# Decoder layer on one core: early attention tiles kept at 32 keys through the value product, and the first cross-attention group prepared inside the feed-forward

## What is computed

```
x  = x + linear_attention(layernorm(x)) @ wo          # 16 heads of 8 features, elu+1 feature map
x  = layernorm(x + gelu_table(layernorm(x) @ w1) @ w2) # feed-forward 128-512-128
s  = where(query_masked or key > query, -1e9, q k^T / sqrt(8))   # q from x, k and v from the context
y  = layernorm(x + softmax(s) v @ WO)
out = layernorm(y + y Wshared + sum(top-2 gates) * (y Wexpert) + bias)
```

## Time and profile before

| | us |
|---|---|
| median of 3 runs | 604.05 (602.84 to 606.14) |
| the profiled execution | 608.8 |
| its span, first to last instruction | 607.1 |
| PE busy | 533.2 (88%) |
| DVE busy | 417.6 (69%) |
| ACT busy | 371.0 (61%) |
| POOL busy | 340.5 (56%) |
| TensorE's mean granted clock | 0.969 |

### The profile page before, as it was taken

One profiled execution on the slowest core, in us unless ns is written; L12 is line 12 of the kernel. 1 busy time (PEld: TensorE's weight loads), 2 busy tenths in 40 slices (PEclk: granted clock), 3 DMA queues, 4 the chain that ended last, 5 costly groups with the idle time before them and its releaser, 6 DMA issues.

```text
span 607.1 us, 23038 instructions
## 1 busy us (share of the span) xinstructions
PE 533.2 (88%) x9312; PEld 371.9 (61%) x9312; DVE 417.6 (69%) x1453; ACT 371.0 (61%) x643; POOL 340.5 (56%) x619
## 2 busy tenths in 40 slices
PE   2799999989999999888999999998989989999741
PEld 1477676756777777635666666666656656666530
DVE  2577777756677766345677797777876887779743
ACT  2365665647777777646666666676666756766521
POOL 6766666656755554531345546754575457544564
PEclk9899999999999999969999999999999999999876
DMA  6600000000000000011111111111111111101001
GB/s 170 181 32 2 3 1 3 3 2 1 1 2 1 2 1 2 9 25 29 32 31 29 42 30 49 39 35 28 49 49 25 27 49 48 28 25 32 20 19 35
DMA packets 24987, 17.97 MB, mean 30 GB/s; under 512 B 3121, under 2 KB 21425, under 8 KB 24881
## 3 DMA queue, kind: packets, MB, share of 16 engines
q1 hardware_dynamic: 24448, 16.43, 10.3%
q10 hardware_dynamic: 432, 0.07, 0.1%
HBM read 9.67 MB, written 4.19 MB: 23 GB/s over the span
## 4 chain that ended last, share of the span: by engine, by line
PE 61%; SPq 11%; issue 7%; POOL 6%; ACT 5%; DMA 5%; DVE 4%; POOLq 0%; DVEq 0%; ACTq 0%
SPq L391 11%; PE pair L1143 7%; PE pair L1127 7%; PE pair L1158 6%; PE pair L1177 6%; PE pair L1210 6%; PE pair L1018 5%; DMA k_exp<-k_sb 4%; PE pair L1096 4%; PE pair L1187 4%; PE pair L1109 3%; PE pair L1196 3%; PE pair L1089 3%; ACT gel L684 3%; PE pair L1165 2%
## 5 line engine op out<-in xcount | busy, mean ns | idle before, releaser
L684 ACT ACTIVATE gel<-pair 128x1024 f32<-128x1024 f32 x64 | 65.6, 1025 | 76.8 <-PE pair L1177 76.8
L908 DVE TENSOR_REDUCE neg_max<-pair 128x16 f32<-128x1024 f32 x64 | 60.9, 952 | 24.5 <-PE pair L1165 24.4
L1158 PE MATMUL pair<-k_exp,qT 64*32 64x256 f32 (+1 forms) x1024 | 58.1, 505 | 13.1 <-DMA k_exp<-k_sb 10.0
L1143 PEld LDWEIGHTS pair<-w,gel 128*128 128x128 f32 x512 | 60.7, 192 | 9.0 <-issue 7.2
L1187 PEld LDWEIGHTS pair<-v,gel 128*32 128x32 f32 x4096 | 41.5, 110 | 36.2 <-ACT gel L684 31.2
L1143 PE MATMUL pair<-w,gel 128*128 128x128 f32 x512 | 62.1, 275 | 1.0 <-ACT gel L650 1.0
L1187 PE MATMUL pair<-v,gel 128*32 128x18 f32 x4096 | 48.0, 187 | 14.1 <-ACT gel L684 11.3
L1127 PE MATMUL pair<-hT,w 128*128 128x512 f32 x128 | 58.5, 597 | 2.0 <-ACT lev L645 1.3
L678 ACT ACTIVATE gel<-gel,row_scale 128x512 f32<-128x512 f32 x80 | 54.4, 720 | 6.3 <-DVE gel L921 6.2
L300 POOL TENSOR_SCALAR veps_c<-mv_c 128x4 f32<-128x4 f32 x16 | 3.7, 230 | 95.4 <-issue 89.0
L1177 PE MATMUL pair<-ident,gel 128*128 128x128 f32 x384 | 52.5, 280 | 0.4 <-ACT gel L678 0.4
(11 more groups left out here) (126 smaller groups left out, 1236.7 us busy)
## 6 DMA issues: line engine op xcount, KB each, us to landing
X<-in_x SPq DMA_DIRECT2D x16, 256.0 KB, 3.0
cT<-in_ctx SPq DMA_DIRECT2D x16, 256.0 KB, 2.9
out_rows<-X SPq DMA_DIRECT2D x16, 256.0 KB, 2.6
k_exp<-k_sb SPq DMA_DIRECT2D x160, 16.0 KB
w<-in_L_attn_w SPq DMA_DIRECT2D x2, 256.0 KB, 3.5
w_kv<-in_L_attn_wk SPq DMA_DIRECT2D x1, 64.0 KB, 3.2
w_q<-in_L_attn_wq ACTq DMA_DIRECT2D x1, 64.0 KB, 3.0
w_kv<-in_L_attn_wv SPq DMA_DIRECT2D x1, 64.0 KB, 3.1
```

What stands on the lines that cost most here:

```text
L684: nc.scalar.activation(pT[par], pair[par][:, :, :].rearrange("p a c -> p (a c)"), ACT.Copy).then_inc(pT_ready, 1)
L908: nc.vector.tensor_reduce(neg_max[par][:, :].rearrange("p (a h) -> p a h", a=2), scores, AX.X, ALU.max, negate=True).then_inc(max_ready, 1)
L1143: last = nc.tensor.matmul(bank(6 + q)[:, P * t:P * (t + 1)], gel[:, q, f, P * t:P * (t + 1)], w_2[:, f, :], start=(f == 0), stop=(f == NF ...
L1158: nc.tensor.matmul(pair[t % 2][b * QW:(b + 1) * QW, half, 0:HH * width], qT[p][rows, batch + first:batch + first + QW], keys, start=True, ...
```

## The change

1. Odd tiles keep 32 keys for each head to the end. The turned probabilities are then 512 columns wide: four transposes and a 128x512 copy in place of eight and 128x1024. The value product takes four heads at a time (`v4`, 36 columns, 16 products). What masked queries owe to the later keys is one product over all heads (144 columns, four products) with a matrix `future`, which DVE makes from a mask row (`mask_rows`) that SP loads for each group. POOL no longer writes future keys; it copies the values of the first 32 keys into `v4` (`spread_v`, four copies a group).
2. The causal term of even tiles is added only to their last 32 keys.
3. PE transposes the rows of the feed-forward's result straight from `X`; POOL's copy of them (`copy_y`, L503) is gone. `yT` and `y2` get other memory.
4. The preparation of group 0 (keys, values, turned rows, queries, first scores) goes into the steps 11 to 15 of `phase2`, on bank 1. ACT's rows_a for the last groups move into the start of `phase3`.
5. In `phase1` DVE makes `phi_q` before `attend`.

```diff
+        v4 = [sb(f"v4{i}", [P, 2 * TG, QB, QB, HV]) for i in range(2)]
-        y2 = sb("y2", [P, TG, D])
+        y2 = xn[0]
...
+            def load_mask(g, p):
+                src = mask_early[2 * g:2 * g + 2, :].rearrange("n p -> (n p)")
+                sp.dma_start(mask_rows[p][:, :, :].rearrange("p n q -> p (n q)"),
+                             src.partition_broadcast(P)).then_inc(mask_loaded[p], 16)
...
                     load_ctx(s + 2, p)
+                if exists(s + 1) and s >= 0:
+                    after(sp, future_ready, s)
+                    load_mask(s + 1, 1 - p)
                 if exists(s - 2):
                     store(s - 2)
...
+            const(nc.gpsimd.memset(late_key[:, :], 0.0))
...
+                const(nc.gpsimd.memset(v4[i][:, :, :, :, :], 0.0))
+                for j in range(QB):
+                    const(nc.gpsimd.memset(v4[i][j * QW:(j + 1) * QW, :, :, j, DH:HV], 1.0))
...
             def phase3(s, p):
-                if exists(s):
-                    future_keys(2 * s + 1)
-                if exists(s + 2) and not early(s):
-                    copy_y(s + 2, p)
                 g, q = s + 1, 1 - p
                 if exists(g):
...
+                if exists(g):
+                    spread_v(g, q)
                 if exists(s - 2):
                     o = s - 2
                     ln_deviation(pool, ln_c, o, mv_c, veps_c, rstd_c)
...
-                nc.scalar.activation(pT[par], pair[par][:, :, :].rearrange("p a c -> p (a c)"),
-                                     ACT.Copy).then_inc(pT_ready, 1)
+                flat = pair[par][:, :, :].rearrange("p a c -> p (a c)")
+                nc.scalar.activation(pT[par], flat[:, 0:GW] if n % 2 else flat, ACT.Copy)\
+                    .then_inc(pT_ready, 1)
...
-            phase3(-1, 1, slots=(0, 1))
-            phase2(NG, 0)
-            phase3(-1, 1, slots=range(2, TG))
-            phase2(NG + 1, 1)
+            rows_a(NG - 3, 1)
+            probabilities(0)
+            rows_a(NG - 2, 0)
             act.wait_ge(down_done, NG)
-            pipeline(act, phase3, first=0, last=NG + 1)
+            phase3(0, 0, slots=(0,))
+            rows_a(NG - 1, 1)
+            phase3(0, 0, slots=range(1, TG))
+            pipeline(act, phase3, first=1, last=NG + 1)
...
-                if exists(s):
-                    attend(s, p)
                 if exists(g):
                     dve.wait_ge(expq_ready, g + 1)
                     after(dve, num_done, g - 1)
                     nc.vector.scalar_tensor_tensor(phi_q[q][:, :], bank(1), 1.0, expqk[q][:, 0, :],
                                                    ALU.add, ALU.max).then_inc(phiq_ready, 1)
+                if exists(s):
+                    attend(s, p)
...
+            def future_keys(g, q):
+
+                dve.wait_ge(mask_loaded[q], g // 2 * 16 + 16)
+                after(dve, pv_done, g * TG - TG)
+                nc.vector.tensor_scalar(future[q][:, :, :], mask_rows[q][:, :, :], 0.0,
+                                        late_key[:, 0:1], ALU.not_equal, ALU.mult)\
+                    .then_inc(future_ready, 1)
+
             def phase3(s, p, slots=range(TG)):
                 prev, old, q = s - 1, s - 2, 1 - p
                 for t in slots:
+                    if t == 2 and exists(s + 1):
+                        future_keys(s + 1, q)
...
+                if s == NG - 5:
+                    pe.wait_ge(projsb_ready, NG)
+                    pe.wait_ge(ctx_loaded[0], 16)
+                    project_qk(cT[0], w_xk, bank(1), xk_done)
+                if s == NG - 4:
+                    pe.wait_ge(k_ready, 1)
+                    project_v(0, 0)
+                if s == NG - 3:
+                    pe.wait_ge(v2_ready, 1)
+                    turn_y(0)
+                if s == NG - 2:
+                    pe.wait_ge(yT_ready, 1)
+                    project_qk(yT, w_xq, bank(1), xq_done)
+                if s == NG - 1:
+                    pe.wait_ge(const_ready, 3)
+                    pe.wait_ge(const_dve, 4)
+                    pe.wait_ge(h2T_ready, NG)
+                    first_scores(0, 0)
...
-                for i in range(HH):
+                for i in range(HH // 2 if n % 2 else HH):
                     if i % (HH // 2) == 0:
                         pe.wait_ge(exp_ready, shifted(n, 2 * i // HH))
...
+                if n % 2:
+                    pe.wait_ge(v4_ready, (n // TG + 1) * QB)
+                    pe.wait_ge(future_ready, n // TG + 1)
+                    for b in range(QB):
+                        nc.tensor.matmul(
+                            bank(7)[b * QW:(b + 1) * QW, 0:H * HV],
+                            future[p][:, t // 2, b * QW:(b + 1) * QW],
+                            v2[p][:, t // 2 * QB + b, :, :, :].rearrange("p i h e -> p (i h e)"),
+                            start=True, stop=False)
+                    for i in range(QB):
+                        for b in range(QB):
+                            last = nc.tensor.matmul(
+                                bank(7)[b * QW:(b + 1) * QW, QB * HV * i:QB * HV * (i + 1)],
+                                pT[1][:, P * i + b * QW:P * i + (b + 1) * QW],
+                                v4[p][:, t // 2 * QB + b, i, :, :].rearrange("p h e -> p (h e)"),
+                                start=False, stop=i == QB - 1)
```

More of the change, by code:

```diff
@@ L266, in up_bank, with first_bank @@
             return (6, 7, 2, 3)[f] if s == 0 else 2 + f
+        def first_bank(g, usual):
+            return 1 if g == 0 else usual
         def shifted(n, half):
@@ L378, in _ @@
             load_ctx(0, 0)
+            load_mask(0, 0)
             def spread_k(g, q):
@@ L494, in phase2, with spread_k @@
                     ln_offset(pool, ln_a, s - 1, mv_b, negm_b, rstd_b[1 - p], offs_b[1 - p])
-            def copy_y(g, p):
-                pool.wait_ge(ln_a.done, g + 1)
-                pool.wait_ge(h2_xposed, NG - 1 if isinstance(g, int) and g == 0 else NG)
-                after(pool, y_xposed, g - 1)
-                apart(pool)
-                nc.gpsimd.tensor_copy(y_in[p][:, :, :], X[:, tiles(g), :]).then_inc(y_copied, 1)
-            def spread_k(g, q, heads):
-                for h in heads:
+            def spread_k(g, q):
+                pool.wait_ge(k_ready, g + 1)
+                after(pool, s_done, g * TG - TG)
+                for h in range(HDMA, HH):
@@ L675, in probabilities @@
                     act.wait_ge(sub_ready, shifted(n, half))
[L676 to L677 removed]
+                    rows = probability_rows(n)
+                    part = rows if n % 2 else rows[:, GW * half:GW * (half + 1)]
                     nc.scalar.activation(part, part, ACT.Exp, scale=row_scale[:, n:n + 1])\
```

207 lines of the change are left out of this document (115 added, 92 removed).

## The result

The changed kernel takes 668.24 us (median of 4 runs, 665.32 to 670.66), the kernel before 605.1 us (median of 4, 602.84 to 610.29): a ratio of 1.1028, 95% interval 1.0943 to 1.1114. It is slower by 10%, where 2% faster (591.3 us) was forecast and 600 us was the upper end of the range. The profiled execution took 667.96 us and has a span of 666.2 us, against 608.8 and 607.1.

A forecast was written before the change was run, and what follows sets the result against it. Each stage had its own limit, cross-attention a closed loop of scores, DVE, POOL, store and ten DMAs. The terms 5.5 − 1.3 − 8.0 − 8.5 − 2.5 + 2 = −12.8 us against the 604.05 us median gave 591.3 us, range 582 to 600.

The forecast's parts named there:

- 0.3 us of mask row: Cross-attention step: DVE's added work for the mask row, priced at 0.3 us, with DVE still free before the scores are done.
- Fills, +5.5: Start: POOL's constant fills delay the first normalisation by 4.7 us, and PE's restart at the lower clock adds 0.8 us.
- `phi_q`, −1.3: Linear attention: making `phi_q` first saves at most 0.1 us in each of 13 steps, 1.3 us in all.
- Seam, −8.0: Feed-forward to cross-attention: 3.3 us of inserted PE work, then 26.4 us to group 1's first scores instead of 37.7.
- Cross-attention, −8.5: First scores of group 1 to those of group 15: 266.4 us where 274.96 us passed before.
- +2 for the clock: Cross-attention: two or three steps with a late DMA run PE at the lower clock, costing 2 us in all.
- PE's work, 17.0 to 17.1: Cross-attention step: PE needs 17.0 to 17.1 us, 2.0 us saved by cheaper odd and even tiles and a shorter wait.
- Tail, −2.5: After group 15's first scores: cheaper odd tiles, a smaller causal term and earlier expert products save 2.5 us.
- The loop is not closed: Rival, cross-attention: the store doesn't hold the DMAs back, steps follow PE at 17.1 us, 567 us in all; chance 0.07.
- The fills are hidden: Rival, start: something else holds the start, so 4.7 us less and no cold restart, 586 us; chance 0.13.
- The first group is not hidden: Rival, seam: late ACT or DVE, low clock or slower `weigh_values` loses 5 to 9 us, 596 to 600 us; chance 0.15.
- The lower clock in every step: Rival, cross-attention: PE restarts at 1.2 GHz after each key wait, steps take 21.0 us, 611 us in all; chance 0.10.

The follow-up runs named there:

- e1: Changed kernel with each group's mask rows loaded one step earlier; 598.71 us, ratio 0.9877 to the kernel before.
- e7: Kernel before with only `phi_q` put ahead of `attend` on DVE; 607.78 us, ratio 1.0018 to the kernel before.
- e3: e1 with the store of a group's result moved behind the ten key DMAs of the following step; 588.13 us, ratio 0.9701 to the kernel before.
- e5: e3 with POOL's fills of the value buffers spread over four steps of linear attention; 582.06 us, ratio 0.9620 to the kernel before.
- e8: e1 with eight key DMAs a step in place of ten; 584.94 us, ratio 0.9662 to the kernel before.
- e9: e5 with eight key DMAs a step in place of ten; 578.58 us, ratio 0.9541 to the kernel before.
- e12: Changed kernel, mask load left late, with DVE's `future_keys` moved from slot 2 to slot 3 behind the shift; 601.62 us, ratio 0.9929 to the kernel before.

## Why the prediction was wrong

The step that failed is one sentence: "SP's mask load stands behind the DMAs and ahead of a store that comes 12 us later". It asks who stands behind the load in SP's list, and prices it at nothing. It does not ask who waits for the load and what is queued behind that wait. The first time was to be had from rows of before: the list begins at the store and the ten DMAs take 6.8 us to issue, so a load behind them lands some 10 us after the store, an estimate (11.2 us in the change, 384.50 to 395.73). In e1, where it waits for nothing, DVE comes to `future_keys` 6.0 us after the store (399.12 to 405.11) or 7.6 (378.95 to 386.59), and the code had it at the head of slot 2, with the shifts behind it. I gave DVE "0.3 us of mask row" and looked at its duration alone. So the wait for the mask rows was put at nothing, and it measured 59.2 us in 15 waits; without it the same kernel is 69.5 us faster (e1). No rival had this case, and the chance of 0.09 for slower had other reasons.

Point by point, with the profiled executions (before to change; e1 where the late load hides a term):

- *Fills, +5.5, and `phi_q`, −1.3.* The last step of linear attention, PE's products with a wait of 1.26 us for ACT, starts at 133.28 in before, at 138.16 in the change: +4.9 (forecast +4.2). The normalisation of group 2 was where forecast, PE's transposes at 28.95 after 6.20 us. `phi_q` gave 0, since ACT's chain to `hT`, and 0.15 us from there to PE, had been the bound all along (e7).
- *Seam, −8.0.* From last `up` products to first scores of group 1: 26.9 us (forecast 26.4). Together with 3.15 us of inserted work (forecast 3.3): −7.6. Right.
- *Cross-attention, −8.5 and +2 for the clock.* First scores of group 1 to those of group 15: 274.96 us in before, 332.46 in the change (276.45 to 608.91): +57.5. In e1 it is 273.57 (276.15 to 549.72), −1.4. The undisturbed loop was right (19.03 us, forecast 19.15; its own terms, 19.1 less 0.11, give 19.0), but the mean step was 19.97 and not 19.45: the 0.3 us for late DMAs and the 2 us for the clock were too small by 12 × 0.52 = 6.2 us. That is nearly all of the 7.4 us between e1 and the forecast.
- *PE's work, 17.0 to 17.1, with the wait for `pT` at 0.1.* Measured 17.34, and 18.53 with its own waits (e3), of which 0.70 us is the one for `pT`. The value product of an odd tile did not get cheaper: 0.45 and 0.48 us of records (L1252, L1259), from the first's start to the end of the second 0.75 us, against 0.74.
- *Tail, −2.5.* In e1 −1.5 (549.72 to 573.77 against 25.54 us). In the change it is 4.3 us longer, with a wait of 3.22 us for ACT behind the last mask load.
- *The rivals.* "The loop is not closed", 567 us: opening it gives 588 (e3), since PE's step is 18.53 and not 17.1. "The fills are hidden": no (e5). "The first group is not hidden": no, the seam gave 7.6 us. "The lower clock in every step", 611 us: not in every step of e1, but in five of eleven. The Trainium skill's rule that I set against the change ("TensorE: Matmul & The Clock Gate", "Loop structure matters more than you think") was nearer to e1 than my 2 us. The change's trace agrees with it in kind: behind a DMA wait, here of 1.60 us, the granted clock is 0.50 from 394.5 to 399 us.

The load's own landing time could be told beforehand: issue to landing has a median of 3.3 us in the change, for 128 KB, and 2.9 us in before for `cT`, 256 KB. The Trainium skill's fit for one DMA ("DMA: Bandwidth & Descriptors", "Anatomy of one DMA — SWDGE (gpsimd) path") gives an estimate of 2.0 + 0.3 = 2.3 us, for DMAs that GpSimd issues and not SyncE; the trace has 1.0 us more.

What stays open: why e8 and e9 come 3 us under e3 and e5 with the same steps was only located and not tested. By the profiled executions, e9 gains 2.6 of its 3.1 us ahead of the full steps; e8, 2.7 us shorter, gains 1.2 us there and 1.9 us behind the last key DMAs, and loses 0.4 in the steps. And why e1 loses the clock in steps where before keeps it (below) was not tried by itself.

## What to carry to other kernels

For each transfer that a change adds, write two times side by side: when it lands, counted from the head of its queue's list, and when its consumer's engine reaches the wait. Then follow what is queued behind that wait until it comes back to the list: if what the wait delays also releases what stands ahead of the load, the wait repeats in every step, here 15 times 3.9 us. A load that needs no result of the step belongs a step ahead, or its request late in the consumer's step.

When a wait is removed, look for a second loop of nearly the same length before crediting the first; an experiment that opens one loop alone can show nothing and still be informative.

One-time work on an idle engine costs nothing only where that engine isn't the next one waited for: the same fills cost about 5 us at the start, made TensorE wait 3.8 us when they stood at the end of linear attention, and cost nothing in steps with 1.9 us idle on POOL.

## What the runs showed of the hardware

TensorE lost its full clock behind some short waits and kept it behind longer ones. In before a wait of 2.28 us in one piece left it at 1.00, in the window up to 456 us and in the next one, the first row below. In e1 a wait of 1.66 us, which stands behind the same value products as in before, was followed by scores of 1.96 us, and the next two windows show the clock around it:

```profile
456.00:460.00 4.00, 3.32 (x94) 2.45 (x87) 3.14 (x6) 2.19 (x4) 0.00 (x0) 1.00 0.00 0
...
404.00:408.00 4.00, 2.07 (x104) 1.85 (x112) 3.66 (x19) 2.33 (x4) 3.22 (x7) 0.96 0.23 44
408.00:412.00 4.00, 3.83 (x40) 1.75 (x28) 2.50 (x6) 1.57 (x4) 1.65 (x4) 0.61 0.24 81
```

In e1 itself a wait of 1.21 us cost nothing, and e12, which does the same work in cross-attention, kept 1.00 through a whole step with a wait of 1.86 us:

```profile
328.73 1.09 PE L1221 MATMUL pair<-k_exp,qT 64*32 64x512 f32 x16 [1.86 <-DMA k_exp<-k_sb]
...
320.10:339.40 19.30, 16.92 (x392) 11.32 (x390) 15.69 (x53) 12.29 (x22) 11.28 (x23) 1.00 0.18 46
```

So the length of one wait does not decide alone, and a forecast that takes the longest harmless wait of one execution as the bound for another kernel, as mine did, is too hopeful. In e3, with waits for the keys of at most 1.34 us, all twelve steps had 1.00.
